# Layer norms and an attention scaling with a repeated scalar as second tensor operand, in a fused graph attention and graph convolution kernel

## What is computed

```python
h = maximum(layernorm(x), 0)                      # layer norm 1
# graph attention, layer 1 (4 heads of 128) and layer 2 (1 head of 256):
xl   = (h @ W).reshape(B, N, H, F)
e    = leaky_relu(asrc[:, :, None, :] + adst[:, None, :, :], 0.2)
attn = softmax(where(mask[..., None], e, -1e9), axis=1)
out  = einsum('bsdh,bshf->bdhf', attn, xl) + bias   # elu between the layers
x = x + out_of_layer_2
h = maximum(layernorm(x), 0)                      # layer norm 2
x = x + h + einsum('bni,doi->bno', h, weights) + take(label_bias, adj).sum(axis=2)

def layernorm(x): return (x - mean(x)) / sqrt(var(x) + 1e-5)   # over the 256 features
```

## Time and profile before

| | before |
|---|---|
| median of 3 runs | 523.75 us (522.41 to 524.24) |
| profiled execution: time | 523.36 us |
| profiled execution: span in the trace | 521.6 us |
| granted TensorE clock, mean | 0.993 |
| PE busy | 488.1 us (94%) |
| DVE busy | 487.1 us (93%) |
| ACT busy | 444.9 us (85%) |
| POOL busy | 386.5 us (74%) |

### The profile page before, as it was taken

The page is one execution under the profiler, slowest core; times in us unless marked ns, Lnnn a source line. Parts: engine busy times, 40 slices in busy tenths (PEclk is TensorE's granted clock), DMA queues, the critical chain, the costliest instruction groups (busy, mean ns, idle before and its releaser), DMA issues.

```text
span 521.6 us, 14585 instructions
## 1 busy us (share of the span) xinstructions
PE 488.1 (94%) x3428; PEld 420.0 (81%) x3428; DVE 487.1 (93%) x1437; ACT 444.9 (85%) x1604; POOL 386.5 (74%) x556
## 2 busy tenths in 40 slices
PE   4498999999999999999999999999999999999875
PEld 1377788888888888888888888888888888888764
DVE  7989999999999999999999999999999999999763
ACT  2378999989999999999999999999999999998841
POOL 3276878878787788887777788878777887877642
PEclk9999999999999999999999999999999999999997
DMA  8110101111110111111101111111011111000011
GB/s 237 37 32 8 33 27 53 54 34 53 51 48 24 51 51 51 46 36 51 51 23 49 51 51 51 31 51 51 23 49 51 51 51 33 20 24 21 23 42 41
DMA packets 29148, 23.72 MB, mean 45 GB/s; under 512 B 1976, under 2 KB 28860, under 8 KB 29120
## 3 DMA queue, kind: packets, MB, share of 16 engines
q1 hardware_dynamic: 27328, 21.44, 13.4%
q10 hardware_dynamic: 1792, 1.98, 1.4%
HBM read 14.56 MB, written 8.39 MB: 44 GB/s over the span
## 4 chain that ended last, share of the span: by engine, by line
PE 47%; DVE 23%; issue 16%; POOL 6%; ACT 5%; ACTq 1%; DVEq 1%; POOLq 0%
DVE hn L704 8%; PE pA L913 6%; PE pY L925 4%; PE pY L926 4%; PE pY L927 4%; PE pA L906 3%; POOL P L345 3%; ACT L L441 3%; DVE nmax L734 3%; DVE L L729 3%; PE pC L950 3%; PE pH L867 2%; PE pZ L898 2%; PE pF L969 2%; PE pZ L895 2%
## 5 line engine op out<-in xcount | busy, mean ns | idle before, releaser
L446 ACT ACTIVATE L<-L,nmax 128x128 f32<-128x128 f32 x256 | 100.1, 406 | 8.8 <-DVE nmax L734 8.8
L329 POOL TENSOR_TENSOR h_lo<-h,h_hi 128x512 fp32r<-128x512 f32 x64 | 83.0, 1297 | 17.3 <-ACT h_hi L500 17.3
L352 POOL TENSOR_TENSOR hT_lo<-hT_f,hT_hi 128x256 fp32r<-128x256 f32 x64 | 47.3, 739 | 42.8 <-ACT hT_hi L429 42.6
L925 PE MATMUL pY<-w_hi,h_hi 128*128 128x258 f32 x256 | 76.5, 299 | 0.9 <-POOL h_lo L329 0.6
L926 PE MATMUL pY<-w_lo,h_hi 128*128 128x258 f32 x256 | 72.6, 283 | 0.0
L927 PE MATMUL pY<-w_hi,h_lo 128*128 128x258 f32 x256 | 72.5, 283 | 0.0
L345 POOL TENSOR_TENSOR P<-L,rsum 128x512 f32<-128x512 f32 x64 | 66.5, 1039 | 6.3 <-DVE rsum L738 6.3
L913 PE MATMUL pA<-PT,xl 128*128 128x128 f32 x512 | 67.6, 275 | 0.5 <-ACT PT L454 0.5
L704 DVE TENSOR_SCALAR hn<-x_all,mv,rstd 128x256 f32 (+1 forms) x64 | 64.5, 1007 | 2.1
L913 PEld LDWEIGHTS pA<-PT,xl 128*128 128x128 f32 x512 | 62.9, 192 | 0.7 <-ACT PT L454 0.7
L446 ACT ACTIVATION_READ_ACCUMULATOR L<-L,nmax 128x1 f32 x256 | 52.2, 204 | 0.0
(11 more groups left out here) (156 smaller groups left out, 1735.7 us busy)
## 6 DMA issues: line engine op xcount, KB each, us to landing
x_all<-in_x SPq DMA_DIRECT2D x32, 256.0 KB, 2.8
out<-x_all SPq DMA_DIRECT2D x32, 256.0 KB, 2.2
adj_all<-in_adj SPq DMA_DIRECT2D x32, 128.0 KB, 2.6
x_all<-in_L_gnn_W ACTq DMA_DIRECT2D x2, 512.0 KB, 5.4
rhs<-lhs SPq DMA_DIRECT2D x64, 6.0 KB
rhs<-lhs SPq DMA_DIRECT2D x64, 1.0 KB
x_all<-in_L_gnn_weights ACTq DMA_DIRECT2D x2, 256.0 KB, 7.7
x_all<-in_L_gnn_att_src ACTq DMA_DIRECT2D x1, 128.0 KB, 6.1
```

What stands on the lines that cost most here:

```text
L329: pool.tensor_tensor(h1_lo[p][:, :, :].rearrange("p a b -> p (a b)"), h1[p][:, :], h1_hi[p][:, :, :].rearrange("p a b -> p (a b)").bitcast ...
L446: last = act.activation(L1[p][:, h, :], L1[p][:, h, :], ACT.Exp, bias=nmax1[p][:, h:h + 1], accum_out=sum1[p][:, h:h + 1])
L925: pe.matmul(pY[:, 0:C2], h1_hi[p][:, k, :], w2_hi[:, k, :], start=(k == 0), stop=False)
```

## The change

Three VectorE instructions are written in another form. In both layer norms `tensor_scalar` with two per-partition scalars (subtract the mean, multiply by the inverse deviation) becomes `scalar_tensor_tensor`: the mean stays a per-partition scalar, and the inverse deviation becomes a second tensor operand, the same column repeated along the free axis by a step of zero. In `normalise2`, `tensor_scalar` with one per-partition scalar becomes `tensor_tensor` with the reciprocal repeated in the same way. Output, buffers, semaphores, and the order on every engine stay as they were; nothing is added or removed.

```diff
-                dve.tensor_scalar(hn[p][:, :], of_graph(x_all, g, D), mv1[:, p, 0:1], rstd1[:, p:p + 1],
-                                  ALU.subtract, ALU.mult).then_inc(s_hn, 1)
+                dve.scalar_tensor_tensor(hn[p][:, :], of_graph(x_all, g, D), mv1[:, p, 0:1],
+                                         rstd1[:, p:p + 1].broadcast_to([128, D]), ALU.subtract, ALU.mult).then_inc(s_hn, 1)
...
-                dve.tensor_scalar(h2n[p][:, :], of_graph(x_all, g, D), mv2[p][:, 0:1], rstd2[p][:, :],
-                                  ALU.subtract, ALU.mult).then_inc(s_h2n, 1)
+                dve.scalar_tensor_tensor(h2n[p][:, :], of_graph(x_all, g, D), mv2[p][:, 0:1],
+                                         rstd2[p][:, :].broadcast_to([128, D]), ALU.subtract, ALU.mult).then_inc(s_h2n, 1)
...
-                dve.tensor_scalar(P2[p][:, :], L2[p][:, :], rsum2[p][:, :], None, ALU.mult).then_inc(s_P2, 1)
+                dve.tensor_tensor(P2[p][:, :], L2[p][:, :], rsum2[p][:, :].broadcast_to([128, 128]), ALU.mult).then_inc(s_P2, 1)
```

## The result

| | before | after |
|---|---|---|
| median | 523.08 us (4 runs) | 532.92 us (532.1 to 533.5, 4 runs) |
| ratio to before | | 1.0185, 95% interval 1.0157 to 1.0213 |
| profiled execution: span | 521.6 us | 530.3 us |
| granted TensorE clock, mean | 0.993 | 0.997 |

531.5 us had been forecast, 520 to 543 as the range.

A forecast was written before the change was run, and what follows sets the result against it. The prediction took a chain of waits through VectorE, POOL and TensorE, repeating every two graphs, as the bound. L704's longer tail, 3.8 us, and POOL held up, 4.4, summed to 8.2 us: 531.5 us forecast, range 520 to 543.

The forecast's parts named there:

- Its first step: On VectorE, the new forms with two SBUF inputs still wait for the POOL instruction under way, as the old ones do.
- the tails: The last piece of a VectorE instruction after the awaited POOL instruction ends: L704 0.14 to 0.27 us, L779 0.08 to 0.15.
- a zero step changes nothing: On VectorE, a column repeated by a zero step is read like any other tensor; no row showed it.
- the loops: Chain of waits through VectorE, POOL and TensorE, repeating every two graphs in 14.79 us; 29 counted in the run.
- L704's tail: Layer norm 1 on the chain ends 0.13 us later behind POOL once in each loop: 29 x 0.13 = 3.8 us.
- POOL held up behind the tails: POOL's L329 ends later and TensorE's L925 waits for it: 0.15 us a loop, bounds 0 and 0.18, 4.4 us.
- L711 was put at nothing: Layer norm 2: L779's wait for POOL takes up its added time, 0 us; without cover 4.5 to 8.3 us.
- One of the signs: In the changed kernel's trace, TensorE's waits for L704 and POOL were to be longer.
- the first (no wait for POOL): Rival: a form with a repeated column does not wait for POOL, TensorE bounds, 500 to 515 us; chance 0.15.
- The second (each piece counts): Rival: VectorE is the one bound and every added piece counts uncovered, 536 to 545 us; chance 0.08.
- The third (the tails come to lie beside the loop): Rival: the loop shifts so that the added tails cost nothing, 522.5 to 525 us; chance 0.13 for no change.
- The fourth: Rival: L704 comes before POOL's L329 and POOL waits instead, 20 us less, 503 us; chance 0.04.

The follow-up runs named there:

- the dense operand: Changed kernel with a constant tile of -1, as many elements as the output, in place of the repeated column in all three instructions: 533.58 us.
- the swapped kernel: Kernel before with layer norm 1 (L704) moved ahead of low_rows1 (L716) in VectorE's list, all forms as before: 527.06 us.
- the PSUM kernels: Column in PSUM: on the kernel before for L779 506.77 us, L704 509.00, both 506.56; on the changed kernel for L779 507.55 us.

## Why the prediction was right

Its first step decided it: whether the new forms still wait for POOL. L630 and L638, two instructions of the start-up that run three times in all, showed the wait and the tails of 0.15 and 0.27 us; the changed kernel has 0.15 and 0.28. That three instructions of the start-up stood for the whole run was in part luck. That a zero step changes nothing was an assumption, and the dense operand bore it out. The Trainium skill's rule (SBUF — State Buffer, Who interferes with whom), by which two SBUF inputs contend with a GpSimd instruction that reads SBUF and at most one outside the two-port modes does not, agrees on both sides: 1.066 us as L704's median with both in SBUF, 0.481 with one in PSUM. It does not agree for POOL's L323, which reads SBUF too: L711 runs under it without a wait (last section), and there the measurement decides.

By terms, in the mean of the loops from 100 to 460 us: L704's tail was put at 0.13 us a loop and measured 0.14. POOL held up behind the tails was taken as 0.15 within 0 to 0.18 and measured 0.06 + 0.09 = 0.15 (0.05 + 0.14 in the one loop of the table); L345's 0.05 and L329's 1.46 us stood in the text. So 0.28 us a loop were forecast and 0.29 to 0.30 measured. That 0.15 was met so closely is in part luck, since it was a choice between 0 and 0.18. The 8.2 us forecast compare with 8.7 between the profiled executions and 9.8 (8.2 to 11.1) between the medians; of the changed kernel's four executions the profiled one was the fastest.

The last line of the sum has a slip. From 531.6 us on an execution that lies 0.4 us under the median, the median follows as 532.0 us, not 531.5.

The 0.41 us of an L704 left alone was read from an instruction that began at 36.60, and the earlier trace rows says that no POOL instruction was under way then. The trace has L345 under way until 36.64. The figure stands all the same: L711 has a median of 0.405 us, and L704 in the swapped kernel 0.402.

L779 was put at nothing beyond L345's delay, 29 x 0.05 = 1.5 us; alone it costs 1.2. L711 was put at nothing, and alone costs 1.1 us (0.5 to 1.8): here a term was wrong. Its undisturbed duration is 0.474 us, at the upper bound given (0.48), and the waits of L779 and L704 took up most of what it added, as the text had it. The step left out that L711's tail, too, falls on POOL: at 297.35 in the changed kernel L359 takes 0.92 us behind it, where 0.81 stood before. But that does not explain the 1.1 us, for with L711 alone in the new form the loop grew by only 0.01 us, 0.3 us in 29 loops. Where the rest is spent stays open.

One of the signs failed. TensorE's waits for L704 and for POOL's L345 were to grow; its weight loads waited 10.6 us for L704 in mid-run (12.8 before) and 4.5 us for L345 (5.1 before). What grew were the waits for L779's result, 28 in place of 3, which came to 1.1 us before:

```profile
PEld pH L867 <- DVE hn L704: 10.6, 28, 0.4
```
```profile
PEld pC L945 <- DVE P L779: 7.3, 28, 0.8
```

None of the kernels with one new form shows this (2, 3 and 8 such waits). It has no price that the runs can show: the loop grew by 0.30 us with all three and by 0.28 with the three added up.

The rivals: the first (no wait for POOL) fell, and its price of 500 to 515 us is what the PSUM kernels reached (506.6 to 509.0), by TensorE's bound, as it was worked out. The second (each piece counts) fell by the share of L704. The third (the tails come to lie beside the loop) fell with the loop's 0.30 us. The fourth, that the order at the lock tips over for 20 us, did not come in the changed kernel. Its price was not tested by itself: the swap wins the race and costs 4.2 us, but it also puts L716 behind L704, while L779 still waits; with L779's wait gone L704 wins the race too, and the kernel is 16.5 us faster.

## What to carry to other kernels

When VectorE and GpSimd are both busy, compare one instruction's smallest and largest duration at one shape. Here the spread of L704, 0.41 to 1.45 us, was a wait that no table of waits lists, and it ended with a GpSimd instruction. Writing the scalar as a second SBUF tensor kept that wait and doubled the piece behind it (0.14 to 0.28 us). What helped was a second operand in PSUM: with the reciprocal written there, at no added instruction, this kernel takes 506.8 us against 523.3 before.

Price a wait by what follows it on its engine as well. A cheap instruction that another engine needs, queued behind a waiting one, left the kernel 4 us slower after a swap that won its race.

## What the runs showed of the hardware

- Not every GpSimd instruction holds VectorE up. L711 takes 0.40 us at 300.72 in the kernel before, and 0.47 at 305.31 after, while POOL's L323, a pow on two columns, is under way for 0.70 us (from 300.64 and from 305.23), if the rough span of a POOL instruction is taken as recorded.
- An undisturbed scalar_tensor_tensor of 256 elements with one per-partition scalar takes 0.474 us, the tensor_scalar with two takes 0.405. A tensor_tensor of 128 takes 0.28 us with its column in SBUF or in PSUM.
- A tail holds up the POOL instruction behind it by about 0.1 us less than its own length: 0.28 us gives 1.46 us for 1.27 (0.19), 0.14 gives 1.32 (0.05), 0.15 gives 1.09 for 1.04 (0.05).
- A column repeated by a zero step and a dense tile of 256 columns take the same time (832 and 833 ns beside POOL, 474 and 473 alone).
